# Joining a sort's sums on GpSimd between its scatters, instead of on VectorE

## The chip, the cores and the metric

One core of a Trainium2 chip. The metric is the device time of one execution in microseconds; of the kernel before three executions were timed, and one more was taken by the hardware profiler. All times inside the kernel are microseconds from the start of that profiled execution's span.

## The reference

A layer of a graph network over 3125 nodes of 256 values and 50000 edges. With xn = layernorm(x):

```python
# edges: src, dst (sorted by dst), one weight d2 for each
x   = cat(xn[src], xn[dst], d2)
msg = silu(layernorm(silu(x @ mW1 + mb1)) @ mW2 + mb2)
agg = segment_sum(msg, src)                      # messages summed by source node
h   = xn + silu(cat(xn, agg) @ uW1 + ub1) @ uW2 + ub2
x   = x + h + linear_attention(xn)               # q, k, v; k and v normalised
x   = x + top2_of_8_experts(layernorm(x))
```

The kernel sums the messages by source node on TensorE, and for that it must have the edges in the order of blocks of source nodes. The edges come sorted by dst. So there is a sort in front of everything else, and the change is in it.

## The kernel before

**Stages.** Up to 55 us: constants, loads, for each edge its place in the sorted order. Then the sort (L1581 on VectorE, L900 on TensorE, L1267 on ScalarE, L725 on GpSimd). Then the source tables (25 tiles: TensorE L885 to L887, ScalarE L1293, VectorE L1610), the key/value stage (25 tiles, from L961), mixing, the edge loop (up to 1150 us), the node update and the experts. Each engine has its own instruction list in a fixed order that is written out by hand; they meet by semaphores alone.

**The sort.** The 50000 edges lie on 125 partitions, 400 to each; they are taken in 16 groups (GROUPS) of 25 columns. For one group:

- VectorE compares (L1586, L1588) and multiplies (L1591, six products) and so makes one-hot matrices for lanes and for places, the latter times each of six values of an edge: dst in a high and a low part, the source row, and the weight in three bf16 parts. These six are the "pieces"; they are exact in bf16.
- TensorE sums 25 products into one PSUM bank (L906): now each edge's pieces stand at its sorted lane and place, 128 lanes x 28 places (PLACES), six times. It then makes the numbers of the chunks where the 7 runs (RUNS) of 128 chunks belong (L912): a product with two columns each, the high and the low part of a start.
- ScalarE copies the six pieces to SBUF (L1272, `pieces`, two sets in turn) and the source row, which is one piece only, straight to `sort_sb` (L1273, signal `sort_ok`).
- VectorE joins in `land(g - 1)`, behind the one-hot matrices of group g: dst = piece 0 + piece 1 (L1570), the weight = piece 3 + piece 4 + piece 5 (L1571, L1572), and the chunk numbers `chunk_to` = high part + low part + row (L1576, L1578, signal `chunk_ok`).
- GpSimd waits for `sort_ok` and `chunk_ok` of the group and issues 7 indirect DMAs (L729), each of which scatters 128 chunks of 48 bytes to DRAM by `chunk_to`; 112 in all.

**Order.** TensorE's bank of group g is free when `sort_ok` and `chunk_ok` of group g - 2 are there (L903). ScalarE's set of pieces is free when `chunk_ok` of group g - 2 is there (L1271). VectorE may overwrite its one-hot matrices when TensorE has summed group g - 2 (L1583). Beside the sort the same loop makes the normalised nodes, their transposes and the table of the destination nodes (two tiles a group; L922, L885 to L887, L840 on TensorE, L1221, L1279, L1285 on ScalarE, L1600 on VectorE).

**After it.** SP loads the scattered records back (L572) when all 112 scatters have landed and `logit0_ok` is there, a signal from tile 7 of the key/value stage (L1667). TensorE asks for the records behind the key/value stage. In the source tables TensorE may be four banks ahead of VectorE (L931); ScalarE waits for TensorE's signal `tab_ps` (L1292).

GpSimd does nothing between the last scatter and 370 us. From there it gathers rows for the edge loop with indirect DMAs too (L763), twelve at first, then four after each two small additions (L748, L750).

Of the kernel before, what the change touches and what calls it, by code (L numbers as in the profile page):

```python
# [4 lines left out]
F32 = mybir.dt.float32  # L5
# [37 lines left out]
def gps_layer(nc, x, src, dst, edge_weight1, mW1, mb1, ln_g, ln_b, mW2, mb2, uW1, ub1, uW2, ub2,  # L43
# [53 lines left out]
    with ctx:  # L97
# [11 lines left out]
        def at(name, shape, dt, owner, byte=0):  # L109

            return nc.alloc_sbuf_tensor_at(name, shape, dt, offset=place[owner] + byte)
# [92 lines left out]
        part_w = sort_use("part_w_t", [128, PLACES], F32)  # L204
        pieces = sort_use("pieces_t", [128, 2, PIECES, PLACES], F32)
# [82 lines left out]
        mixP_byte = filled["weights"] - 4 * QC * D  # L288
        k_n.append(at("k_n2", [128, NQ], F32, "weights", mixP_byte))
# [44 lines left out]
        run_to = s("run_to", [128, RUNS])  # L334
# [56 lines left out]
        def bank(b, n=512, rows=128, first=0):  # L391
# [16 lines left out]
        scattered, table_ps = sem("scattered"), sem("table_ps")  # L408
# [31 lines left out]
        gap_ok, exp_ok, hotk_ok, route_ps, tile_ok = (sem(n) for n in (  # L440
            "gap_ok", "exp_ok", "hotk_ok", "route_ps", "tile_ok"))
# [97 lines left out]
        def _(sp):  # L539
# [44 lines left out]
            sp.wait_ge(chunk_ps, GROUPS)  # L584
# [68 lines left out]
        def _(pool):  # L653
# [70 lines left out]
            pool.wait_ge(zeros_out, 16)  # L724
            for g in range(GROUPS):  # L725
                pool.wait_ge(sort_ok, g + 1)
                pool.wait_ge(chunk_ok, g + 1)
                for j in range(RUNS):
                    pool.indirect_dma_start(  # L729
                        out=sorted_edges, out_offset=bass.IndirectOffsetOnAxis(chunk_to[:, g, j:j + 1], 0),  # L730
                        in_=sort_sb[:, g, j].rearrange("p c f -> p (c f)"), in_offset=None).then_inc(scattered, 16)
# [106 lines left out]
        def _(pe):  # L838
# [61 lines left out]
            for g in range(GROUPS):  # L900
                pe.wait_ge(sort_in, SORT_IN * (g + 1))
                if g >= 2:
                    pe.wait_ge(sort_ok, g - 1)  # L903
                    pe.wait_ge(chunk_ok, g - 1)
                for c in range(GC):
                    m = pe.matmul(bank(g % 2, PIECES * PLACES), lane_hot_e[0:NP, g % 2, c // 2, :, c % 2],  # L906
                                  place_val[0:NP, g % 2, c // 2].rearrange("p v t b -> p (v t) b")[:, :, c % 2],
                                  start=(c == 0), stop=(c == GC - 1))
                m.then_inc(sort_ps, 1)
                pe.wait_ge(reached_ok, g + 1)  # L910
                for j in range(RUNS):
                    m = pe.matmul(bank(4 + g % 2, 2, first=2 * j), reached[0:NB + 1, g % 2, j * 128:j * 128 + 128],  # L912
                                  group_h[0:NB + 1, g, :], start=True, stop=True)
                m.then_inc(chunk_ps, 1)
                for t in TILES_OF[g]:
                    pe.wait_ge(fills, PADS)
                    pe.wait_ge(w_lo_ok, MW1_LO)
                    pe.wait_ge(xnT_lo_ok, t + 1)
                    if t >= 2:
                        pe.wait_ge(dst_sb, t - 1)  # L920
                    pe.wait_ge(fills, BW_CUT)
                    pe.matmul(bank(6 + t % 2, D), bw_sel[:], bw_cut[:], start=True, stop=False)  # L922
                    first_layer(bank(6 + t % 2, D), t, 1).then_inc(dst_ps, 1)
                for t in TILES_OF[g + 1]:
                    turn_xn(t)
# [299 lines left out]
        def _(act):  # L1225
# [41 lines left out]
            for g in range(GROUPS):  # L1267
# [3 lines left out]
                after(act, chunk_ok, g - 1)  # L1271
                A(pieces[:, g % 2].rearrange("p v t -> p (v t)"), bank(g % 2, PIECES * PLACES), ACT.Copy)  # L1272
# [145 lines left out]
            act.wait_ge(gap_ok, 1)  # L1418
            A(wtmp[0:NP], wtmp[0:NP], ACT.Exp).then_inc(exp_ok, 1)
# [49 lines left out]
        def _(dve):  # L1469
# [97 lines left out]
            def land(g):  # L1567
                dve.wait_ge(sort_ok, g + 1)
                piece = lambda v: pieces[:, g % 2, v].rearrange("p (j c) -> p j c", c=CHUNK)
                st.did(dve.tensor_tensor(sort_sb[:, g, :, :, 0], piece(0), piece(1), ALU.add))  # L1570
                step(dve.tensor_tensor(part_w[:].rearrange("p (j c) -> p j c", c=CHUNK), piece(3), piece(4), ALU.add))  # L1571
                st.did(dve.tensor_tensor(sort_sb[:, g, :, :, 2], part_w[:].rearrange("p (j c) -> p j c", c=CHUNK),  # L1572
                                         piece(5), ALU.add))
                dve.wait_ge(chunk_ps, g + 1)
                ends = bank(4 + g % 2, 2 * RUNS).rearrange("p (j h) -> p j h", h=2)
                st.did(dve.tensor_tensor(run_to[:], ends[:, :, 0], run_row[:], ALU.add))  # L1576
                st.join()
                dve.tensor_tensor(chunk_to[:, g], ends[:, :, 1], run_to[:], ALU.add).then_inc(chunk_ok, 1)  # L1578

            st.join()  # L1580
            for g in range(GROUPS):  # L1581
# [20 lines left out]
                if g:  # L1602
                    land(g - 1)
            land(GROUPS - 1)
# [247 lines left out]
            dve.tensor_tensor(wtmp[R], top_v[R, :, 1], top_v[R, :, 0], ALU.subtract).then_inc(gap_ok, 1)  # L1852
# [34 lines left out]
            dve.wait_ge(exp_ok, 1)  # L1887
# [118 lines left out]
```

## Time and profile before

| what | value |
|---|---|
| median of 3 runs | 1540.53 us (1538.51 to 1542.7) |
| profiled execution | 1532.65 us |
| its span, first to last instruction | 1530.9 us |
| TensorE, VectorE, ScalarE, GpSimd busy | 1302.3, 1154.1, 904.1, 866.8 us |
| granted clock of TensorE, mean | 0.918 |

The busy time of an engine is the time in which an instruction of it runs; the issue of a DMA by SP is not counted, an indirect DMA on GpSimd is, for as long as GpSimd makes its descriptors. In the timelines below a row is: start, duration, engine, line, operation, output<-inputs, shapes, and in brackets how long the engine was idle before it and what ended that ("issue": nothing that the profile shows; "remote": a signal whose sender it cannot name).

### The profile page before, as it was taken

What the parts mean: (1) busy time and instruction counts of PE and PEld (TensorE: products, weight loads), DVE (VectorE), ACT (ScalarE), POOL (GpSimd) and SP (SyncE); (2) the same over time, 40 slices, a digit from 0 to 9 for tenths busy, and PEclk for the clock granted to TensorE, in tenths of its full rate; (3) what the DMA queues carried; (4) which work ended last, traced back from release to release, by engine and by line L of the source; (5) the groups of instructions that cost most, each with busy time, mean ns of one, the idle gap of its engine ahead of it and who ended that gap; (6) DMA issues with size and microseconds to landing.
All of it is one profiled execution on the core that took longest, in us unless ns stands there. A gap on an engine that the chain in (4) does not pass through costs nothing.

```text
span 1530.9 us, 31977 instructions
## 1 busy us (share of the span) xinstructions
PE 1302.3 (85%) x8639; PEld 1135.4 (74%) x8640; DVE 1154.1 (75%) x2784; ACT 904.1 (59%) x1796; POOL 866.8 (57%) x960
## 2 busy tenths in 40 slices
PE   2576727998789999999999999999998956999991
PEld 1365626887678888888888888888886745888891
DVE  6975815884279989999999999999994678766662
ACT  1843603442257777777777777777774553666660
POOL 2287870002277777777777777777760012676761
PEclk7676967998879999999999999999999987999996
DMA  3911100001123333333333333333354143444447
GB/s 131 163 27 25 43 14 8 15 3 41 41 87 103 94 93 93 93 102 97 90 93 93 102 93 94 92 95 100 94 66 165 41 149 138 66 72 75 73 64 265
DMA packets 69786, 129.87 MB, mean 85 GB/s; under 512 B 22626, under 2 KB 43424, under 8 KB 69095
## 3 DMA queue, kind: packets, MB, share of 16 engines
q0 software_dynamic: 35408, 74.18, 20.5%
q1 hardware_dynamic: 33538, 51.70, 11.7%
q10 hardware_dynamic: 780, 3.24, 0.5%
q8 instruction: 31, 0.51, 0.1%
q14 instruction: 29, 0.24, 0.1%
HBM read 103.71 MB, written 25.22 MB: 84 GB/s over the span
## 4 chain that ended last, share of the span: by engine, by line
PE 51%; DVE 15%; ACT 11%; issue 10%; another core or an unknown queue 7%; DMA 3%; DVEq 1%; ACTq 1%; POOLq 0%; SPq 0%
PE ps L840 9%; ACT msg1n_t L1353 7%; PE ps L1079 5%; PE ps L1057 3%; PE ps L1052 3%; PE ps L1053 3%; PE ps L1069 3%; PE ps L1180 2%; DVE place_val_t L1591 2%; PE ps L1209 2%; PE ps L1211 2%; PE ps L1210 2%; PE ps L1181 2%; PE ps L1182 2%
## 5 line engine op out<-in xcount | busy, mean ns | idle before, releaser
L763 POOL DMA_INDIRECT msg_t<-dst_table,stage_idx x424 | 422.7, 997 | 121.1 <-issue 119.5
L1052 PE MATMUL ps<-w_hi_t,msg1T_hi_t 128*128 128x256 f32 x848 | 239.3, 304 | 0.0
L1353 ACT ACTIVATE msg1n_t<-msg_t,nw_b,nw_y 128x256 f32<-128x256 f32 x424 | 229.3, 591 | 0.0
L1079 PE MATMUL ps<-msg_t,hot_t 128*125 128x256 f32 x848 | 222.4, 384 | 2.0 <-issue 0.9
L1053 PE MATMUL ps<-w_lo_t,msg1T_hi_t 128*128 128x256 f32 x848 | 221.6, 283 | 0.0
L1360 ACT ACTIVATE msg_t<-ps 128x512 f32<-128x512 f32 x212 | 125.5, 592 | 124.0 <-remote 100.6
L1748 DVE TENSOR_TENSOR msg_t<-ps,msg_t 128x512 f32<-128x512 f32 x212 | 144.4, 681 | 63.3 <-remote 59.4
L1726 DVE TENSOR_TENSOR agg_t<-agg_t,ps 125x256 f32 x424 | 173.6, 409 | 6.8 <-PE ps L1079 3.4
L1057 PE MATMUL ps<-w_hi_t,msg1T_lo_t 128*128 128x256 f32 x848 | 171.0, 283 | 0.0
L1053 PEld LDWEIGHTS ps<-w_lo_t,msg1T_hi_t 128*128 128x128 f32 x848 | 163.1, 192 | 0.0
L1341 ACT ACTIVATE msg1T_hi_t<-ps 128x512 fp32r<-128x512 f32 x212 | 126.4, 596 | 60.4 <-PE ps L840 56.0
L1052 PEld LDWEIGHTS ps<-w_hi_t,msg1T_hi_t 128*128 128x128 f32 x848 | 161.9, 191 | 0.0
L1079 PEld LDWEIGHTS ps<-msg_t,hot_t 128*125 128x125 f32 x848 | 143.4, 187 | 21.0 <-issue 6.4
L840 PEld LDWEIGHTS ps<-ident,msg1n_t 128*128 128x128 f32 x848 | 97.4, 141 | 75.6 <-ACT msg1n_t L1353 52.4
L840 PE MATMUL ps<-ident,msg1n_t 128*128 128x128 f32 x848 | 134.6, 282 | 21.7 <-ACT msg1n_t L1353 19.1
L729 POOL DMA_INDIRECT sorted_edges<-sort_sb_t,chunk_to x112 | 128.0, 1143 | 37.3 <-issue 32.6
L1743 DVE BATCH_NORM_STATS2 est<-msg_t 128x6 f32<-128x512 f32 x212 | 147.5, 696 | 2.1 <-ACT msg_t L1346 2.1
L1735 DVE SCALAR_TENSOR_TENSOR msg1T_lo_t<-ps,msg1T_hi_t 128x512 fp32r<-128x512 f32 x212 | 144.4, 681 | 4.6 <-issue 2.4
L1346 ACT ACTIVATE msg_t<-msg_t 128x512 f32<-128x512 f32 x212 | 133.7, 631 | 12.4 <-DVE msg_t L1748 11.4
L1057 PEld LDWEIGHTS ps<-w_hi_t,msg1T_lo_t 128*128 128x128 f32 x848 | 132.1, 192 | 0.0
L1069 PE MATMUL ps<-src_hi_t,hotT_t 127*128 x424 | 114.3, 290 | 8.4 <-DVE hotT_t L1708 8.4
L831 POOL DMA_INDIRECT total<-slot_z,to_row x56 | 88.6, 1582 | 48.9 <-ACT slot_z L1433 44.3
(373 smaller groups left out, 3098.8 us busy)
## 6 DMA issues: line engine op xcount, KB each, us to landing
near_rows<-row_list SPq DMA_DIRECT2D x42, 320.0 KB
w_sb_t<-in_L_ffn_W_dram SPq DMA_DIRECT2D x16, 512.0 KB, 8.7
msg_t<-dst_table,stage_idx POOLq DMA_INDIRECT x424
res_t<-in_x_dram SPq DMA_DIRECT2D x1, 3125.0 KB
total<-zero_chunks_t SPq DMA_DIRECT2D x1, 3125.0 KB
dst_table<-dst_stage SPq DMA_DIRECT2D x25, 125.0 KB
xm_table<-xm_t POOLq DMA_DIRECT2D x5, 625.0 KB, 7.6
sum_a_t<-total SPq DMA_DIRECT2D x5, 625.0 KB, 10.7
```

The costliest lines, as they stand in the source:

```text
L763: pool.indirect_dma_start(out=msg1[:, k, j, :], out_offset=None, in_=dst_table, in_offset=bass.IndirectOffsetOnAxis(stage_idx[:, G * k + j ...
L840: return pe.transpose(out_, in_, ident[0:rows, 0:rows])
L1052: pe.matmul(o[j], part(msg1T_hi, j, c), w2_hi[:, c, :], start=(c == 0), stop=False)
L1053: pe.matmul(o[j], part(msg1T_hi, j, c), w2_lo[:, c, :], start=False, stop=False)
L1057: m = pe.matmul(o[j], part(msg1T_lo, j, c), w2_hi[:, c, :], start=False, stop=(c == KD - 1))
L1069: m = pe.matmul(bank(1 + k % 2, D, first=j * D), hotT[0:HR, k, j * 128:j * 128 + 128], table[0:HR, bass.ts(blk[k, j], 1), :].rearrange("p ...
L1079: m = pe.matmul(bank(7 * (kl % 2), D, rows=NP, first=j * D), hot[:, kl % 2, j, 0:NP], msg2[:, kl % 2, j, :], start=True, stop=True)
L1353: m = A(msg1n[:, (kl + 1) % 2, j, :], msg1[:, kk, j, :], ACT.Identity, bias=nw_b[:, kk, j:j + 1], scale=nw_y[:, kk, j:j + 1])
L1726: dve.tensor_tensor(a, a, bank(7 * ((k + 1) % 2), D, rows=NP, first=j * D), ALU.add).then_inc(sum_sb, 1)
L1735: dve.scalar_tensor_tensor(msg1T_lo[:, k % 2], bank(3 + k % 2), 1.0 / ROOT_D, msg1T_hi[:, k % 2].bitcast(F32), ALU.add, ALU.subtract).then ...
L1743: dve.bn_stats(est_pairs[:, kk, :], msg1[:, kk].rearrange("p j n -> p n j")).then_inc(spread_ok, 1)
L1748: dve.tensor_tensor(v, bank(1 + k % 2), v, ALU.add).then_inc(pre_sb, 1)
```

## The change

The three additions of `land` go from VectorE to GpSimd's list, between the scatters. For each group GpSimd runs three parts, one addition each; behind each part it issues scatters of earlier groups: 2, 2 and 1 up to group 8, from there 3, 4 and 3 (at most those of groups that are joined; so 3, 4, 1 in group 14, 3, 4, 0 in group 15, none in group 0), and at the end the last 7. A new semaphore `landed` counts joined groups. The pieces get six sets instead of two; ScalarE waits for `landed` of six groups ago instead of `chunk_ok` of two groups ago. The six sets lie where a later stage's `mixP` is; the third key buffer, which was there, moves to the start of that region. The high and the low part of the chunk numbers are summed by TensorE in PSUM (14 products of one column instead of 7 of two), and VectorE makes one addition of them instead of two. SP no longer waits for `chunk_ps`. Two semaphores of a much later stage (`gap_ok`, `exp_ok`) are made one.

```diff
-        part_w = sort_use("part_w_t", [128, PLACES], F32)
-        pieces = sort_use("pieces_t", [128, 2, PIECES, PLACES], F32)
+        part_w = at("part_w_t", [128, 2, PLACES], F32, "work", 15872)
+        PIECE_SETS = 6
...
+        pieces = at("pieces_t", [128, PIECE_SETS, PIECES, PLACES], F32, "weights", filled["weights"] - 4 * QC * D)
+        k_n.append(at("k_n2", [128, NQ], F32, "weights"))
...
@@ GpSimd
+            def land(g, part):
+                piece = pieces[:, g % PIECE_SETS]
+                if part == 0:
+                    pool.wait_ge(sort_ok, g + 1)
+                    st.did(pool.tensor_tensor(part_w[:, g % 2], piece[:, 3], piece[:, 4], ALU.add))
+                if part == 1:
+                    st.did(pool.tensor_tensor(sort_sb[:, g, :, :, 0], in_chunks(piece[:, 0]), in_chunks(piece[:, 1]), ALU.add))
+                if part == 2:
+                    st.join()
+                    pool.tensor_tensor(sort_sb[:, g, :, :, 2], in_chunks(part_w[:, g % 2]), in_chunks(piece[:, 5]), ALU.add)\
+                        .then_inc(landed, 1)
+
+            def scatter(g, j):
+                pool.wait_ge(landed, g + 1)
+                pool.wait_ge(chunk_ok, g + 1)
+                pool.indirect_dma_start(
+                    out=sorted_edges, out_offset=bass.IndirectOffsetOnAxis(chunk_to[:, g, j:j + 1], 0),
+                    in_=sort_sb[:, g, j].rearrange("p c f -> p (c f)"), in_offset=None).then_inc(scattered, 16)
+
+            sent = 0
             for g in range(GROUPS):
-                pool.wait_ge(sort_ok, g + 1)
-                pool.wait_ge(chunk_ok, g + 1)
-                for j in range(RUNS):
-                    pool.indirect_dma_start(
...
+                for part in range(3):
+                    land(g, part)
+                    upto = min(sent + (2 - part // 2 if g < 9 else 3 + part % 2), RUNS * g)
+                    for q in range(sent, upto):
+                        scatter(q // RUNS, q % RUNS)
+                    sent = max(sent, upto)
+            for q in range(sent, GROUPS * RUNS):
+                scatter(q // RUNS, q % RUNS)
@@ TensorE
                 for j in range(RUNS):
-                    m = pe.matmul(bank(4 + g % 2, 2, first=2 * j), reached[0:NB + 1, g % 2, j * 128:j * 128 + 128],
-                                  group_h[0:NB + 1, g, :], start=True, stop=True)
+                    for h in range(2):
+                        m = pe.matmul(bank(4 + g % 2, 1, first=j), reached[0:NB + 1, g % 2, j * 128:j * 128 + 128],
+                                      group_h[0:NB + 1, g, h:h + 1], start=(h == 0), stop=(h == 1))
@@ ScalarE
-                after(act, chunk_ok, g - 1)
-                A(pieces[:, g % 2].rearrange("p v t -> p (v t)"), bank(g % 2, PIECES * PLACES), ACT.Copy)
+                after(act, landed, g + 1 - PIECE_SETS)
+                A(pieces[:, g % PIECE_SETS].rearrange("p v t -> p (v t)"), bank(g % 2, PIECES * PLACES), ACT.Copy)
@@ VectorE
-            def land(g):
-                dve.wait_ge(sort_ok, g + 1)
-                piece = lambda v: pieces[:, g % 2, v].rearrange("p (j c) -> p j c", c=CHUNK)
-                st.did(dve.tensor_tensor(sort_sb[:, g, :, :, 0], piece(0), piece(1), ALU.add))
-                step(dve.tensor_tensor(part_w[:].rearrange("p (j c) -> p j c", c=CHUNK), piece(3), piece(4), ALU.add))
-                st.did(dve.tensor_tensor(sort_sb[:, g, :, :, 2], part_w[:].rearrange("p (j c) -> p j c", c=CHUNK),
-                                         piece(5), ALU.add))
+            def chunk_places(g):
                 dve.wait_ge(chunk_ps, g + 1)
-                ends = bank(4 + g % 2, 2 * RUNS).rearrange("p (j h) -> p j h", h=2)
-                st.did(dve.tensor_tensor(run_to[:], ends[:, :, 0], run_row[:], ALU.add))
-                st.join()
-                dve.tensor_tensor(chunk_to[:, g], ends[:, :, 1], run_to[:], ALU.add).then_inc(chunk_ok, 1)
+                dve.tensor_tensor(chunk_to[:, g], bank(4 + g % 2, RUNS), run_row[:], ALU.add).then_inc(chunk_ok, 1)
```

## Rows read from the trace of the kernel before

**Rows 1.** Stretches: PE, PEld, DVE, ACT, POOL busy (instructions), clock, DMA share, GB/s

```profile
100.00:165.00 65.00, 44.51 (x265) 36.86 (x265) 36.03 (x83) 25.97 (x57) 51.59 (x45) 0.70 0.11 27
165.00:198.00 33.00, 27.44 (x263) 23.81 (x261) 27.12 (x71) 17.55 (x40) 26.40 (x22) 0.97 0.16 40
198.00:240.00 42.00, 7.17 (x26) 5.99 (x27) 5.12 (x10) 3.13 (x9) 26.86 (x28) 0.53 0.06 10
257.00:352.00 95.00, 91.96 (x493) 78.16 (x492) 75.90 (x169) 44.35 (x74) 0.00 (x0) 1.00 0.03 10
```

**Rows 2.** Waits from 55 to 198 us (two) and from 198 to 300 us (one)

```profile
DVE xnT_lo_t L1600 <- issue: 26.9, 8, 5.9
...
ACT pieces_t L1272 <- remote: 24.2, 7, 4.9
...
ACT src_hi_t L1293 <- remote: 37.7, 5, 15.7
```

**Rows 3.** The chain that ended last, 216 to 257 us: start, duration, what

```profile
216.52 15.69 another core or an unknown queue
...
232.62 5.90 another core or an unknown queue
...
256.83 0.47 PE ps L961
```

**Rows 4.** Timeline of GpSimd: the first scatter, two in the sort, the last

```profile
71.34 1.95 POOL L729 DMA_INDIRECT sorted_edges<-sort_sb_t,chunk_to  x1 [3.45 <-DVE chunk_to L1578]
...
186.69 1.99 POOL L729 DMA_INDIRECT sorted_edges<-sort_sb_t,chunk_to  x1 [0.30 <-issue]
...
191.78 0.96 POOL L729 DMA_INDIRECT sorted_edges<-sort_sb_t,chunk_to  x1 [0.30 <-issue]
...
232.23 0.96 POOL L729 DMA_INDIRECT sorted_edges<-sort_sb_t,chunk_to  x1 [0.31 <-issue]
```

**Rows 5.** Timeline of VectorE in the sort, groups 6, 12, 14 and 15

```profile
98.64 1.88 DVE L1586 TENSOR_TENSOR lane_hot_e_t<-pair_iota_t,edge_h_t 125x3328 bf16<-125x3328 bf16 x1
...
166.76 1.88 DVE L1586 TENSOR_TENSOR lane_hot_e_t<-pair_iota_t,edge_h_t 125x3328 bf16<-125x3328 bf16 x1
...
179.56 1.88 DVE L1586 TENSOR_TENSOR lane_hot_e_t<-pair_iota_t,edge_h_t 125x3328 bf16<-125x3328 bf16 x1
...
185.27 0.18 DVE L1570 TENSOR_TENSOR sort_sb_t<-pieces_t 128x28 f32<-128x28 f32 x1
...
185.95 1.88 DVE L1586 TENSOR_TENSOR lane_hot_e_t<-pair_iota_t,edge_h_t 125x3328 bf16<-125x3328 bf16 x1
...
188.32 2.77 DVE L1591 TENSOR_TENSOR place_val_t<-place_hot_t,edge_h_t 125x728 bf16<-125x728 bf16 x6
...
196.27 0.17 DVE L1578 TENSOR_TENSOR chunk_to<-ps,run_to 128x7 int32<-128x7 f32 x1
```

**Rows 6.** Timelines: VectorE's six products of group 1, GpSimd's subtraction beside them

```profile
63.70 5.47 DVE L1591 TENSOR_TENSOR place_val_t<-place_hot_t,edge_h_t 125x728 bf16<-125x728 bf16 x6
...
64.39 2.52 POOL L722 TENSOR_TENSOR mw_lo_t<-mw_sb,mw_hi_t 128x1024 fp32r<-128x1024 f32 x1 [4.24 <-ACT mw_hi_t L1266]
```

**Rows 7.** Timelines: gather runs on GpSimd, and who waits at their end

```profile
374.11 0.97 POOL L763 DMA_INDIRECT msg_t<-dst_table,stage_idx  x1 [2.17 <-issue]
...
386.64 0.94 POOL L763 DMA_INDIRECT msg_t<-dst_table,stage_idx  x1 [0.30 <-issue]
...
388.32 0.42 DVE L1696 TENSOR_TENSOR res_t<-res_t,ps 125x256 f32<-125x256 f32 x1 [8.13 <-remote]
...
577.30 1.03 POOL L763 DMA_INDIRECT msg_t<-dst_table,stage_idx  x1 [0.17 <-issue]
...
582.27 0.21 POOL L748 TENSOR_TENSOR nw_v<-est,eps_sum 128x4 f32<-128x4 f32 x1
...
583.04 0.60 ACT L1360 ACTIVATE msg_t<-ps 128x512 f32<-128x512 f32 x1 [1.45 <-remote]
```

**Rows 8.** Timeline of SP: the load of the scattered records

```profile
293.40 0.25 SPq L572 DMA_DIRECT2D table_in_t<-sorted_edges  x1
```

More of the change, by code:

```diff
@@ L287, in gps_layer @@
         uw1_sb = at("uw1_sb", [128, KD, D], F32, "weights", filled["weights"] - 4 * QC * D)
-        mixP_byte = filled["weights"] - 4 * QC * D
-        k_n.append(at("k_n2", [128, NQ], F32, "weights", mixP_byte))
+        pieces = at("pieces_t", [128, PIECE_SETS, PIECES, PLACES], F32, "weights", filled["weights"] - 4 * QC * D)
+        assert 4 * PIECE_SETS * PIECES * PLACES <= 4 * QC * D
+        k_n.append(at("k_n2", [128, NQ], F32, "weights"))
         mixG_hi = w("mixG_hi", [128, KD, D], F32R)
@@ L333, in gps_layer @@
         run_row = s("run_row", [128, RUNS])
-        run_to = s("run_to", [128, RUNS])
         token = s("token", [128, TOPK * NB])
@@ L407, in gps_layer @@
             "reached_ok", "sort_in", "sort_ps", "sort_ok", "chunk_ps", "chunk_ok"))
-        scattered, table_ps = sem("scattered"), sem("table_ps")
+        scattered, landed, table_ps = sem("scattered"), sem("landed"), sem("table_ps")
         table_sb, side_out, xnT_lo_ok, w_hi_ok, w_lo_ok = (sem(n) for n in (
@@ L439, in gps_layer @@
             "var2_ok", "sd2_ok", "rstd2_ok", "xm_ok", "x2T_ps", "x2T_sb", "logit_ps"))
-        gap_ok, exp_ok, hotk_ok, route_ps, tile_ok = (sem(n) for n in (
-            "gap_ok", "exp_ok", "hotk_ok", "route_ps", "tile_ok"))
+        softmax_ok, hotk_ok, route_ps, tile_ok = (sem(n) for n in ("softmax_ok", "hotk_ok", "route_ps", "tile_ok"))
+        GAP_OK, EXP_OK = 1, 2
         logit_ok = sem("logit_ok")
@@ L583, in _ @@
             sp.wait_ge(chunk_ok, GROUPS)
-            sp.wait_ge(chunk_ps, GROUPS)
             sp.wait_ge(zeros_out, 16)
@@ L724, in _ @@
             pool.wait_ge(zeros_out, 16)
-            for g in range(GROUPS):
-                pool.wait_ge(sort_ok, g + 1)
-                pool.wait_ge(chunk_ok, g + 1)
-                for j in range(RUNS):
-                    pool.indirect_dma_start(
-                        out=sorted_edges, out_offset=bass.IndirectOffsetOnAxis(chunk_to[:, g, j:j + 1], 0),
-                        in_=sort_sb[:, g, j].rearrange("p c f -> p (c f)"), in_offset=None).then_inc(scattered, 16)
+            in_chunks = lambda t: t.rearrange("p (j c) -> p j c", c=CHUNK)
+            def land(g, part):
[16 more added lines that the diff above has]
+            sent = 0
+            for g in range(GROUPS):
+                for part in range(3):
[6 more added lines that the diff above has]
+                scatter(q // RUNS, q % RUNS)
             pool.wait_ge(table_sb, LOADS)
@@ L1417, in _ @@
                 copy_xm(t, t // 4 + 1)
-            act.wait_ge(gap_ok, 1)
-            A(wtmp[0:NP], wtmp[0:NP], ACT.Exp).then_inc(exp_ok, 1)
+            act.wait_ge(softmax_ok, GAP_OK)
+            A(wtmp[0:NP], wtmp[0:NP], ACT.Exp).then_inc(softmax_ok, 1)
             act.wait_ge(w2_in, 16 * NE)
@@ L1602, in _ @@
                 if g:
-                    land(g - 1)
-            land(GROUPS - 1)
+                    chunk_places(g - 1)
+            chunk_places(GROUPS - 1)
             dve.wait_ge(zeros_out, 16)
@@ L1851, in _ @@
             st.join()
-            dve.tensor_tensor(wtmp[R], top_v[R, :, 1], top_v[R, :, 0], ALU.subtract).then_inc(gap_ok, 1)
+            dve.tensor_tensor(wtmp[R], top_v[R, :, 1], top_v[R, :, 0], ALU.subtract).then_inc(softmax_ok, 1)
             for k in range(TOPK):
@@ L1885, in _ @@
             st.did(dve.tensor_copy(slot_t[R], slot_q[R, 1]))
-            dve.wait_ge(exp_ok, 1)
+            dve.wait_ge(softmax_ok, EXP_OK)
             step(dve.tensor_scalar(wgt[R, 0, :], wtmp[R], 1.0, None, ALU.add))
```

## The prediction

> **What bounds the kernel now.** I read the stretches first [rows 1]. The change touches nothing behind the key/value stage; all that can move lies before it, in the sort (56 to 196 us), the source tables (to 257 us) and the key/value stage (to 352 us). Two of the stretches are strange. From 198 to 240 us TensorE works 7.2 of 42 us, VectorE 5.1 and ScalarE 3.1, while GpSimd is the only engine that is never free (28 scatters). From 100 to 165 us VectorE too works only 36.0 of 65 us; in the 33 us behind it, with the same work in a group, 27.1.
>
> The waits say who is late [rows 2]. ScalarE waits 37.7 us in five waits for TensorE's signal that a source table is in PSUM; in the sort it waits 24.2 us for the pieces in the same way, and VectorE 26.9 us in front of L1600. The chain [rows 3] puts 15.69 us and 5.90 us of this on nobody ("another core or an unknown queue"): TensorE had long done the work. The signal itself is late, and it stays late as long as the scatters run: the last scatter starts at 232.2 us [rows 4], the chain moves again at 232.2 and 238.5 us and then at full speed, so that the key/value stage starts at 256.8 us.
>
> What the scatters do in those times is in GpSimd's timeline [rows 4]. Undisturbed, one starts every 1.265 us (0.96 busy, 0.30 between). While VectorE builds the one-hot tensors without a pause, a scatter now and then is held (1.99 us behind the 1.88 us comparison of L1586), four fit in a group of 6.4 us (179.56 to 185.95 us from one comparison to the next, [rows 5]), and nobody's signal is late. The same pattern comes back twice with the gathers [rows 7]: in the run that goes without a pause from 374.1 to 387.6 us VectorE waits 8.13 us, until 0.7 us after its end; and in the edge loop, where four gathers (577.3 to 582.3 us) are followed by two short GpSimd additions, ScalarE waits 1.45 us and gets its signal at 583.04, 0.8 us after the fourth. So my reading is: a run of indirect DMAs without a pause keeps TensorE's signals back from about the third or fourth on, and a pause lets them go. It also explains why the sort falls from 6.4 to 11 or 13 us a group: once VectorE idles, the scatters run without a pause, and that keeps VectorE idle.
>
> **The change, part by part.**
>
> *VectorE.* It loses the three piece additions and one of the two index additions. From the start of L1570 to the next comparison is 0.68 us [rows 5]; one instruction of some 0.15 us stays: 0.5 us a group saved. Against it, an addition on GpSimd that reads SBUF excludes VectorE's two-input instructions: beside the 2.52 us subtraction of L722 six products took 5.47 us [rows 6] instead of 2.77 [rows 5], the whole 2.5 us more. An addition of 28 elements lies between 0.21 us (4 elements, L748, [rows 7]) and 2.52 us (1024 elements); worked out along the line between them 0.26 us. Three a group give back 0.8 us. Net: 6.4 us becomes 6.5 us a group (bounds 5.9, if none is felt, and 7.2, if each costs double).
>
> The Trainium skill, "SBUF — State Buffer", section "Who interferes with whom", has a rule that speaks against the change: a VectorE instruction with two SBUF inputs and a GpSimd instruction that reads SBUF shut each other out for a whole instruction. The trace agrees, with the 5.47 us. By the rule alone, with nothing won at the signals, a group would be some 0.2 us longer and the kernel 3 us slower; that is the last rival below.
>
> *TensorE.* 14 products of one column for 7 of two in each group. No row here has one alone; they lie between nothing and, as the largest bound, the same again as all 44.5 us of TensorE's work shared over its 265 products [rows 1], 0.17 us each, 1.2 us for seven; they are far smaller than the mean product, so I take 0.3 us a group, under VectorE's 6.5 us, and nothing on the path where TensorE is not the bound (16 x 0.3 = 5 us if it were everywhere).
>
> *The sort's pace.* Between the comparisons of groups 6 and 12 there are 68.1 us (98.64 to 166.76, [rows 5]) for six groups; at 6.5 us 39 us: 29 us saved. TensorE's clock there averages 0.70, and 0.97 behind it [rows 1]; if it stayed low, TensorE would bound a group with its own 44.5 us of work in 65 us, or 7.8 us in each 11.35 us group, and 21 us would be left. I take 28: TensorE is busy most of the time when its signals aren't late, and had the high clock of 0.97 from 165 us on, at 6.4 us a group. The last index is then written at 168 us instead of 196.3 us [rows 5].
>
> *GpSimd's own chain.* Up to group 8 it sends five scatters and makes three additions a group: 5 x 1.265, 3 x (0.26 and a little more pause) = 7.2 us, and held by VectorE as now (6.4 less 4 x 1.265 us, so 1.3 us in each group) and at the additions, about 9.8 us. That is slower than the sort; the six sets of pieces are the buffer. Starting at about 75 us (group 0 sends nothing), group 8 is done at 153 us and group 9 is joined at about 162; the pieces of group 15, which need its set, come at 166. Just enough; at 11 us a group the sort would wait about 6 us. Then 72 scatters are left: 91 us, 21 additions 6 us, the waits on its own signal and VectorE's holds 7 us: end at about 257 us, against 233.2 now. The table load waits for that and for L1667; it is issued at 293.4 us now [rows 8] and TensorE asks for it only behind the key/value stage, 352 us. So the 24 us more of GpSimd are hidden, if the signals get through beside them.
>
> *The source tables.* Now 60 us; the 21 tables done when the signals are free take 18.3 us (238.5 to 256.83, [rows 3]), 25 take 22. The scatters now come in runs of 3, 4 and 3 with an addition between. As in the edge loop a signal is held up by 1 to 1.5 us in a run of four; four banks ahead hide part of it: I add 5 us. Key/value starts at 168 + 22 + 5 = 195 us, 62 us earlier.
>
> *The key/value stage.* It takes 95 us for 25 tiles [rows 1], TensorE busy for 92 of them: little slack. Until 257 us it now runs beside scatters, 16 tiles; a signal late by 1.45 us, as in the edge loop, for not quite every second tile is 0.6 us each, 10 us. The last seven scatters have no addition between them; by the run of twelve gathers that cost 8.1 us, some 4 us. Loss 14 us (bounds 3, if the delays fall where there is slack, and 26, if each tile loses 1.4 us).
>
> *The rest* (two semaphores made one, the third key buffer moved, the dropped wait of SP) changes no instruction on the path: nothing. Scatter waits added to each scatter are met before it and cost what the first scatter of a group pays today, no more than the others (0.30 us).
>
> Sum: 62 - 14 = 48 us. The profiled execution took 1532.65 us (span 1530.9 and 1.75 around it), so 1484.6; it is 7.9 us below the median of 1540.5, against which I state 1492.
>
> **The rivals.**
>
> *An addition is too short a pause* (slower). The release in the edge loop came 0.8 us behind the fourth gather, inside a break of 1.6 us; here the break is 0.17 + 0.26 us, little over the 0.30 us that a scatter leaves anyway. If it frees nothing, only GpSimd's wait on its own signal, once in ten scatters, does. From 168 us on the stage crawls until GpSimd ends at 257, and frees itself 5 us later (as 233.2 to 238.5 now). Six breaks of 3 us let 18 of the tables' 22 us pass; key/value starts at 266 us instead of 257: 1550, and up to 1564 if these breaks free nothing either. It decides as soon as signals pass in less than about a quarter of the time (22 of 89 us). The Trainium skill, "GPSIMD Engine Reference", section 4.1, says to leave elementwise additions to VectorE, about twice as fast; only this rival makes those 48 additions count, since then GpSimd's chain is the kernel's. Chance 0.18.
>
> *Half of it*: signals pass about half the time from 168 to 257 us. 45 us of work are done in 89, then 22 + 23 us of it lie behind at 257, so key/value in effect starts at 234: 23 us won, 1518. For it: the scatters' long run freed itself only 5.3 us behind its end (233.2 to 238.5), the run of twelve gathers after 0.7, so scatters seem to keep signals back more tightly. Chance 0.23.
>
> *The buffer runs dry*: at 11 us or more a group on GpSimd the sort ends 6 to 10 us later; 1500. Chance 0.06.
>
> *It isn't the scatters that keep the signals back*, but something of these stages: then only VectorE's part is left, from 4 us gained to 3 us lost. Against it: the three places above. 1540. Chance 0.05.
>
> *Forecast*: 1492, alone 1478 to 1506. Chance 0.48.
>
> **The numbers.** 0.3% is 4.6 us, about what a measurement here can tell. Faster: 0.48 + 0.23 + 0.06, less a little of the half case, 0.76; same 0.07; slower 0.17. The range of 8 in 10 runs from 1476 (sort at 5.9 us a group, tables without delay, a loss of 6 us: 16 us better than the sum) to 1545, into the slower case.
>
> **What the profile after would show.** Right: groups of some 6.5 us through the sort with the last L1578 near 168 us; L961 starting near 195; no wait of ScalarE at the tables over 2 us; GpSimd's last scatter near 257. Wrong: waits "remote" of 5 us and more between additions (first rival); the last scatter's end and the start of L961 close together (half); ScalarE waiting for GpSimd at L1272 (buffer); groups 6 to 11 at 8 us and more with a low clock.

## The result, and the profile after

The changed kernel takes 1551.84 us (median of 20 executions, 1546.93 to 1558.18) beside 1541.8 us for the kernel before (20, 1536.01 to 1553.66): ratio 1.0059, 95% interval 1.0043 to 1.0076, 10 us slower. The profiled execution has a span of 1550.6 us. I had forecast 1492.

The stretches of the changed kernel, columns as in [rows 1]:

```profile
100.00:165.00 65.00, 54.81 (x575) 47.54 (x576) 53.53 (x103) 39.82 (x88) 56.16 (x57) 0.95 0.16 43
165.00:198.00 33.00, 4.51 (x20) 3.72 (x18) 0.85 (x2) 1.15 (x3) 26.22 (x33) 0.55 0.07 12
198.00:240.00 42.00, 4.95 (x18) 4.07 (x18) 3.65 (x5) 1.15 (x3) 30.99 (x40) 0.50 0.03 5
257.00:352.00 95.00, 90.10 (x502) 77.51 (x503) 74.06 (x165) 45.21 (x79) 0.00 (x0) 1.00 0.03 10
```

The sort did what was forecast: in the first stretch VectorE is busy for 53.5 us where it had 36.0, TensorE for 54.8 where it had 44.5, at a clock of 0.95 instead of 0.70. Behind it everything all but stands still, from 165 us to GpSimd's end, twice as long as before. ScalarE's timeline in the source tables shows each signal of TensorE that came:

```profile
165.04 0.38 ACT L1246 ACTIVATE dst_stage<-ps 125x256 f32<-125x256 f32 x1 [4.11 <-remote]
172.57 0.38 ACT L1318 ACTIVATE src_hi_t<-ps 125x256 fp32r<-125x256 f32 x1 [7.15 <-remote]
185.17 0.38 ACT L1318 ACTIVATE src_hi_t<-ps 125x256 fp32r<-125x256 f32 x1 [12.22 <-remote]
201.27 0.38 ACT L1318 ACTIVATE src_hi_t<-ps 125x256 fp32r<-125x256 f32 x1 [15.72 <-remote]
218.07 0.38 ACT L1318 ACTIVATE src_hi_t<-ps 125x256 fp32r<-125x256 f32 x1 [16.42 <-remote]
234.87 0.38 ACT L1318 ACTIVATE src_hi_t<-ps 125x256 fp32r<-125x256 f32 x1 [16.42 <-issue]
247.53 0.38 ACT L1318 ACTIVATE src_hi_t<-ps 125x256 fp32r<-125x256 f32 x1 [12.27 <-remote]
253.16 1.21 ACT L1318 ACTIVATE src_hi_t<-ps 125x256 fp32r<-125x256 f32 x4 [5.25 <-remote]
```

That is six tables in 80 us, 13 to 17 us apart, and the others only behind GpSimd's end; before, five of these waits made 37.7 us [rows 2]. GpSimd's timeline at the start and at the end of that time:

```profile
164.13 0.26 POOL L731 TENSOR_TENSOR part_w_t<-pieces_t 128x28 f32<-128x28 f32 x1
164.56 0.98 POOL L742 DMA_INDIRECT sorted_edges<-sort_sb_t,chunk_to  x1 [0.17 <-issue]
165.84 0.97 POOL L742 DMA_INDIRECT sorted_edges<-sort_sb_t,chunk_to  x1 [0.30 <-issue]
167.11 0.96 POOL L742 DMA_INDIRECT sorted_edges<-sort_sb_t,chunk_to  x1 [0.30 <-issue]
168.09 0.26 POOL L733 TENSOR_TENSOR sort_sb_t<-pieces_t 128x28 f32<-128x28 f32 x1
...
177.29 0.26 POOL L731 TENSOR_TENSOR part_w_t<-pieces_t 128x28 f32<-128x28 f32 x1
...
240.71 0.98 POOL L742 DMA_INDIRECT sorted_edges<-sort_sb_t,chunk_to  x1 [3.90 <-remote]
...
248.32 0.96 POOL L742 DMA_INDIRECT sorted_edges<-sort_sb_t,chunk_to  x1 [0.30 <-issue]
```

Look at the gaps between scatters: an addition (0.26 us) and 0.16 us stand in the place of the 0.30 us that a scatter leaves anyway. Ten scatters and three additions take 13.16 us (from the row at 164.13 to that at 177.29), 1.315 us a scatter, against 1.265 without additions. The additions freed nothing. Even GpSimd's own signal, of its last addition, let it go on only after 3.90 us (0.28 us in e1_join below), and no table passed in that pause either. The last scatter starts at 248.3 instead of 232.2 us [rows 4], ScalarE goes on 3.9 us behind its end, and the key/value stage starts at 269.3 instead of 256.8 us [rows 3]:

```profile
269.30 0.47 PE L986 MATMUL ps<-wkvT_hi_t,xnT_hi_t 128*128 128x512 f32 x1 [1.13 <-DVE src_lo_t L1626]
```

So the sort gained 33 us (its last index at 162.9 instead of 196.3) and the tables lost 46: 12.5 us later in all, which agrees with the 10 us of the medians. (The two profiled executions differ by 19.7 us: that of the kernel before was 9 us under its median of 20. What is left lies behind the key/value stage, where the change touches nothing.)

### The profile page after: what moved, and what is told of

Same layout as the page of the kernel before. It is cut to its first block, busy times and chain, and to the rows that moved or that the text cites. A ratio compares the mean times of both kernels' runs of the same rounds, so it can differ in the third digit from the quotient of the medians.

```text
span 1550.6 us, 32278 instructions
## 1 busy us (share of the span) xinstructions
PE 1290.2 (83%) x8751; PEld 1124.7 (73%) x8752; DVE 1146.5 (74%) x2720; ACT 902.0 (58%) x1796; POOL 881.8 (57%) x1008
## 4 chain that ended last, share of the span: by engine, by line
PE 50%; DVE 15%; ACT 11%; issue 10%; another core or an unknown queue 10%; DMA 3%; DVEq 1%; ACTq 1%; POOLq 0%; SPq 0%
PE ps L864 8%; ACT msg1n_t L1378 7%; PE ps L1104 6%; PE ps L1082 3%; PE ps L1077 3%; PE ps L1078 3%; PE ps L1094 3%; DVE place_val_t L1607 3%; PE ps L1205 2%; PE ps L1234 2%; PE ps L1236 2%; PE ps L1235 2%; PE ps L1206 2%; PE ps L1207 2%
## 5 line engine op out<-in xcount | busy, mean ns | idle before, releaser
L742 POOL DMA_INDIRECT sorted_edges<-sort_sb_t,chunk_to x112 | 123.0, 1098 | 31.4 <-issue 26.6
```

## The experiments

The kernel before was measured again on nine further occasions, each on one core of some chip, beside the kernels below. On six of them it took 1404.2 to 1406.5 us, on three 1530.7 to 1543.8. Traces of both kinds tell what differs: I say "signals on time" and "signals late"; the first result above is of the late kind. 14 of the 18 runs met signals on time, four late ones. The four late ones stand on one execution each, but for h2_join_pace256 (four); what they gain is 60 us and more, where executions of one kernel lie within some 10 us (within 18 us in the first result).

**The kernel before and the changed one, unchanged** (signals on time).

> The kernel before, unchanged, for its trace on this chip. If the late signals belong to the chip and not to the program, a chip on which the kernel before takes about 1406 us shows no wait of ScalarE at the source tables over 1 us although the scatters run without a pause; then its key/value stage starts near 185 us instead of 256.8, and the stage behind the tables waits for nothing. If they belong to the program, the five waits of 4 us and more stand in every trace of it, also in a short one, and the 135 us are lost somewhere else.

> The changed kernel, unchanged. On a chip that does not hold the signals back there is nothing for the change to free and nothing that it can hold longer: the additions stand off VectorE's path (0.5 us in each of 16 groups, 8 us) and give 0.8 us a group back to it; my theory says within 5 us of the kernel before (1402 to 1411). On a chip like that of the first result: 10 us slower again, 1552. The rival, that the additions themselves cost the 10 us (GpSimd's port, VectorE's two-input instructions), says 10 us slower on either.

Measured beside a kernel before of 1404.8 us: b1_before 1409.6 (one execution), a1_after 1405.05, ratio 1.0000 (0.9991 to 1.0008). The stretch from 198 to 240 us of the kernel before:

```profile
198.00:240.00 42.00, 41.22 (x227) 35.33 (x226) 34.75 (x84) 19.42 (x33) 30.06 (x31) 1.00 0.04 6
```

and its row of the 25 tables (durations in ns: least, median, most; first and last start):

```profile
L1293 ACT ACTIVATE src_hi_t<-ps x25: 373/383/402, 168.3 to 188.8; 125x256 fp32r<-125x256 f32 x25
```

TensorE works 41.2 of 42 us where it worked 7.2 [rows 1], beside the same scatters, 1.26 to 1.51 us apart. The 25 tables take 20 us. So the late signals are no property of the program; where there is no wait to free, the two kernels are equal. The same row of the changed kernel:

```profile
L1318 ACT ACTIVATE src_hi_t<-ps x25: 373/383/402, 163.4 to 185.3; 125x256 fp32r<-125x256 f32 x25
```

It begins 5 us earlier (the execution of the kernel before in this comparison was 5 us over its median), though VectorE wrote its last index 13.8 us earlier, at 153.3 us. ScalarE's timeline shows why:

```profile
161.12 0.31 ACT L1297 ACTIVATE pieces_t<-ps 128x168 f32<-128x168 f32 x1 [9.48 <-POOL sort_sb_t L736]
```

Six sets of pieces are too few at five scatters a group, and that takes back what the shorter groups gave, as the next experiment shows. (In the first trace the same wait is there, 7.5 us up to 160.53, 0.1 us behind group 9's third addition at 160.18.)

**The additions back on VectorE** (all else of the change stays), signals on time.

```diff
-                    land(g, part)
...
+            def land_dve(g):
...
             def chunk_places(g):
+                land_dve(g)
```

> The changed kernel with the three additions of a group back on VectorE; one-column products, single index addition and six sets of pieces stay. GpSimd then sends nothing but scatters. If the additions between the scatters let the sort's signals through (groups of 5.9 us instead of 11), on a chip that holds signals back the sort falls back to 9 to 11 us a group and the time to about 1535 to 1545, as before; on a chip that does not, it is 1400 to 1410. If it is one of the other edits that speeds the sort up, the groups stay at 6 us on both.

1402.35, ratio 0.9988 (0.9976 to 1.0001); a second time (one execution) 1403.6 beside 1404.95 (again on time, so that its question stays open):

> The same kernel as e5_adds_back (the three additions back on VectorE), once more. Where signals are held back and it is the additions between the scatters that let the sort through: groups 7 to 12 take 9 us and more again, 1530 to 1550. If the sort keeps 6 us a group, one of the other edits (one-column products, single index addition) did that. The tables crawl in either case. Where they are not held back: 1402 again.

Groups of its sort take 6.27 us from comparison to comparison, those of the changed kernel 5.88 on average (92.60 to 145.49 for nine), those of the kernel before 6.4 us and more:

```profile
101.21 1.88 DVE L1611 TENSOR_TENSOR lane_hot_e_t<-pair_iota_t,edge_h_t 125x3328 bf16<-125x3328 bf16 x1
107.48 1.88 DVE L1611 TENSOR_TENSOR lane_hot_e_t<-pair_iota_t,edge_h_t 125x3328 bf16<-125x3328 bf16 x1
```

(the kernel with the additions back), and of the changed kernel:

```profile
98.48 1.88 DVE L1602 TENSOR_TENSOR lane_hot_e_t<-pair_iota_t,edge_h_t 125x3328 bf16<-125x3328 bf16 x1
104.42 1.87 DVE L1602 TENSOR_TENSOR lane_hot_e_t<-pair_iota_t,edge_h_t 125x3328 bf16<-125x3328 bf16 x1
```

So the three additions are worth 0.4 us a group on VectorE. But the tables start at 161.0 us with the additions back, 2.4 us earlier than in the changed kernel (163.4): its sort is 6 us longer (last index at 159.6 us), but no piece waits for GpSimd. Where signals are on time, the move buys nothing.

**GpSimd waits for its own signal behind every addition**, signals on time.

```diff
                         .then_inc(landed, 1)
+                    pool.wait_ge(landed, g + 1)
+                else:
+                    st.join()
```

> The changed kernel, but GpSimd waits for its own signal behind each of the 48 additions. Rate theory: the scatters, one in 1.27 to 1.32 us, overrun something that serves one in about 1.5 to 1.6 us; while it is behind, the signals of TensorE (and GpSimd's own) wait. Then each wait lasts until it has caught up, some 1 us after three or four scatters, TensorE's signals pass there, the source tables run, and L986 starts at 185 to 200 us instead of 269: 1490 to 1515 us. Break theory: nothing passes until about 4 to 5 us after the last scatter, however few there were before; then each wait is 4 us, GpSimd ends at about 330 us instead of 249 and the kernel takes 1540 to 1580 us. Third theory: only VectorE's dense comparisons keep the scatters harmless, pauses on GpSimd do nothing: 1552 us as now.

1405.64 beside 1406.51, ratio 0.9993 (0.9975 to 1.0010). The gap behind an addition becomes 0.28 us instead of 0.16; no signal was late that it could have freed, so it says nothing of the three theories in its expectation.

**A clear ahead of each scatter.** A `memset` of a scratch tile on GpSimd, 512 columns (0.5 us) or 256 (0.3 us), ahead of each scatter from the 42nd on; it waits for the clear two before it alone. Two further kernels put the same filler in lumps: e4_lump ten clears of 512 columns where `q % 10 == 0`, e6_break4 three where `q % 4 == 1`.

```diff
             def scatter(g, j):
+                q = g * RUNS + j
+                if q > 40:
+                    pause(512)
                 pool.wait_ge(landed, g + 1)
```

> The changed kernel with a memset of 512 elements on GpSimd (about 0.5 us) in front of each scatter from the 42nd on: one scatter in about 1.7 us instead of 1.32. Rate theory: that is slower than what serves them, so no signal is held, L986 starts at about 180 us, and the last scatter at about 272 us is what the table load waits for: 1465 to 1485 us. Break theory: breaks of 0.7 us free nothing, GpSimd ends 22 us later and the kernel takes 1570 to 1575 us. Third theory: 1570 to 1575 us too.

> The same with 256 elements (about 0.3 us): one scatter in about 1.47 us. Rate theory: near the rate at which they are served, so signals are late in part; between 1475 and 1530 us. Break and third theory: GpSimd ends 10 us later, 1560 to 1565 us.

> The changed kernel with the same pause as with 512 elements, but in one piece of about 5.3 us after every ten scatters from the 50th on. Rate theory: the scatters overrun again within each ten, and signals pass only in the break and the first two or three scatters after it, about a third of the time: L986 at 210 to 235 us, 1505 to 1530 us. Break theory: a break over 4 us frees the signals, for 1.3 us in each 18 us: 1555 to 1575 us. Third theory: 1575 us.

> The changed kernel with a break of three clears of 512 columns (0.5 us each, 1.6 us) ahead of every fourth scatter from the 41st on, 18 breaks, 29 us more on GpSimd. If a break of 1.6 us frees the signals, as in the edge loop, a chip that holds them back shows no wait of ScalarE over 4 us from 165 us on and gains 30 us and more against the changed kernel (1500 to 1520). If only a lower rate or the end of the run frees them, it is 25 to 30 us slower than the changed kernel (1575). On a chip that does not hold them back: only GpSimd's end is later, 0 to 15 us slower than before, as with the other pauses.

All four met signals on time, e6_break4 beside 1404.8, the others beside 1406.5: 1418.5 (ratio 1.0084), 1407.4 (1.0006), 1419.0 (1.0088), 1417.1 (1.0089). With no late signal to free they measure two other things. One is GpSimd's slack: with its last scatter at 264.4 us (256 columns) the clears cost nothing; with it at 278.8 us (512 columns), SP issues the load of the records only at 282.4 us, and ScalarE waits for it, 12 us in all:

```profile
ACT side_w_t L1350 <- DMA table_in_t<-sorted_edges: 11.2, 1, 11.2
```

The other is that clears in a row hold VectorE. In e6_break4 nobody waits for the load (last scatter at 273.6 us), yet from first to last tile (`kv_ss`) the key/value stage takes 101.1 us where the changed kernel takes 92.1; in e4_lump it takes 105.0. There an instruction of VectorE that takes 0.40 us otherwise lasts until the ten clears beside it are done; five such instructions cost 13 us in all. A row of GpSimd's timeline and one of VectorE's:

```profile
275.14 4.73 POOL L744 MEMSET scratch_t<- 128x512 bf16 x10
275.55 4.48 DVE L1662 TENSOR_SCALAR res_t<-res_t,res_scale,res_shift 125x256 f32<-125x256 f32 x1
```

The two kernels with a clear ahead of each scatter, once more:

> The same kernel as e2_pace512 (a clear of 0.5 us ahead of every scatter from the 41st on), once more, in the hope of a chip on which the kernel before takes about 1541 us. There, if a lower rate of scatters frees the signals, no wait of ScalarE is over 4 us from 165 us on and the time is 1490 to 1510; if only a whole pause of a microsecond and more or the end of the run does, it is 1570 to 1580. On a chip on which the kernel before takes 1405 us it is 1418 again and says nothing new.

> The same kernel as e3_pace256 (a clear of 256 columns ahead of each scatter from the 41st on: one scatter in 1.475 us instead of 1.315), once more. Where the kernel before takes about 1541 us: if the bound is a rate between 1.315 and 1.475 us a scatter, the waits of ScalarE at the source tables are all under 2 us and the time is 1465 to 1475, since GpSimd ends 14 us earlier than with the clear of 512 columns (1482); if it lies between 1.475 and 1.695 us, some signals are late by 5 us and more and it is 1500 to 1560. Where the kernel before takes 1405 us: 1407 again.

These met late signals: 1482.05 beside 1543.8 (1490 to 1510 was expected if a lower rate frees the signals), and 1464.5 beside 1530.7 (1465 to 1475 was expected). That the executions themselves were of the late kind is seen in their edge loops: from 560 to 900 us ScalarE waits 57.3 and 52.4 us for signals of a sender that the profile cannot name, 52.6 us in the kernel before of the first result, and no such wait is listed for b1_before and a1_after. In h1_pace512 the row of the tables:

```profile
L1329 ACT ACTIVATE src_hi_t<-ps x25: 377/384/406, 164.6 to 186.6; 125x256 fp32r<-125x256 f32 x25
```

and GpSimd's timeline:

```profile
220.61 0.97 POOL L753 DMA_INDIRECT sorted_edges<-sort_sb_t,chunk_to  x1 [0.17 <-issue]
221.58 0.54 POOL L744 MEMSET scratch_t<- 128x512 bf16 x1
222.28 0.97 POOL L753 DMA_INDIRECT sorted_edges<-sort_sb_t,chunk_to  x1 [0.16 <-issue]
```

In h3_pace256 the row of the tables:

```profile
L1329 ACT ACTIVATE src_hi_t<-ps x25: 373/383/402, 164.7 to 186.2; 125x256 fp32r<-125x256 f32 x25
```

and the stretch from 198 to 240 us:

```profile
198.00:240.00 42.00, 40.92 (x223) 34.98 (x223) 34.55 (x80) 19.77 (x34) 37.20 (x63) 1.00 0.03 5
```

With 512 columns the scatters start 1.66 us apart at the least, 2.0 in mean beside the tables and 1.76 behind them; with 256 columns 1.45 us at the least, 1.7 and 1.55 in mean. Neither holds anything back: the tables take 22 us with no wait of ScalarE over 1.8 us, and TensorE works 40.9 of 42 us behind them, although no break is longer than about 1 us. Scatters 1.315 us apart in mean (the changed kernel) hold nearly everything back. So what the additions lacked is room between the scatters. Not separated by these runs is whether the distance of neighbours counts, the mean over several scatters, or that something stands in every gap and not in three of ten.

**The kernel before with the same clears, and nothing of the change** (256 columns, from the 12th scatter on).

> The kernel before, with nothing of the change, and the clear of 256 columns (0.3 us) ahead of each scatter from the 12th on. Where signals are held back: if the scatters' rate is the whole cause, its sort goes at 6.4 us a group too, the tables and the key/value stage run through, and it is 1465 to 1480, as fast as the changed kernel with the same clears (1464.5); if the additions between the scatters are needed for the sort, groups stay at 9 to 11 us and it is 1490 and more. Where they are not held back: 1405 to 1410.

> The same kernel as b2_before_pace256 (the kernel before with a clear of 0.3 us ahead of each scatter from the 12th on), once more, where its first run met signals that were on time. Where the kernel before takes 1531 to 1544 us: 1465 to 1480 if the scatters' rate is the whole cause and nothing of the change is needed; 1490 and more, with groups of 9 to 11 us in the sort, if the additions between the scatters are.

With signals on time 1405.4, ratio 0.9999 (0.9981 to 1.0016). With late ones 1471.4 beside 1532.45 (one execution each), 61 us faster; 1465 to 1480 was expected if the scatters' rate is the whole cause. Its scatters are 1.45 us apart at the least, in mean 1.63 beside the tables and 1.50 behind them. Its tables:

```profile
L1303 ACT ACTIVATE src_hi_t<-ps x25: 374/384/407, 171.6 to 193.5; 125x256 fp32r<-125x256 f32 x25
```

Here the sort goes at 6.4 to 8.4 us a group from group 6 to group 12 (11.35 on average before [rows 5]) with all additions on VectorE. So of the 66 us by which h3_pace256 is faster than the kernel before, the room between the scatters alone gives some 61.

**Joins first: one scatter behind each addition** instead of up to four, so that the pieces' sets come free in time; then the same with the clear of 256 columns from the 46th scatter on.

```diff
-                    upto = min(sent + (2 - part // 2 if g < 9 else 3 + part % 2), RUNS * g)
+                    upto = min(sent + 1, RUNS * g)
```

> The changed kernel with one scatter instead of up to four behind each addition, so that GpSimd joins the pieces as they come and has more scatters left behind the sort. In the changed kernel group 15's pieces wait 7.5 to 9.5 us for the set of group 9, whose last addition stands behind four scatters (160.18, 160.53 us): six sets are too few at five scatters a group. Where signals are not held back: that wait is gone, the sort ends near 152 us, the tables start 8 to 10 us earlier, time 1394 to 1399 beside 1405. Where they are held back: the tables' signals still wait for the scatters' end, which does not move or moves 5 us earlier; 1545 to 1555. The rival for the first case, that GpSimd does not bound the sort, says 1405.

> Joins first, as in e7_join_first (one scatter behind each addition), and the clear of 256 columns ahead of each scatter from the 45th on. Where signals are held back: the sort ends 8 us earlier than in h1_pace512 and the tables run through; 1458 to 1470 if 1.475 us a scatter is slow enough, about 1530 to 1550 if not. Where they are not: 1400 to 1403, since GpSimd ends at about 265 us and so not much later than the 249 us that cost nothing.

e7_join_first, signals on time: 1400.7 beside 1405.7, ratio 0.9953 (0.9933 to 0.9972), 5 us faster; 1394 to 1399 was expected. ScalarE's wait for GpSimd is gone, but the tables start at 157.8 us, 5.6 earlier than in the changed kernel and not 8 to 10. h2_join_pace256, signals late: 1460.5 beside 1530.7, ratio 0.9532 (0.9509 to 0.9554), 70 us faster, the best version (1458 to 1470 was expected):

```profile
L1329 ACT ACTIVATE src_hi_t<-ps x25: 372/383/407, 160.5 to 182.8; 125x256 fp32r<-125x256 f32 x25
```

It was not run where signals are on time.

**Distance or mean rate.** e4_lump was to tell whether the mean over some tens of microseconds counts.

> The same kernel as e4_lump (ten clears of 512 columns, 4.9 us, behind each ten scatters), once more. GpSimd's work is that of h1_pace512 (1482 where the kernel before took 1544), in lumps. If the mean rate counts, it is 1480 to 1490 where signals are held back. If a backlog builds up within ten scatters 1.3 us apart, ScalarE waits 5 to 10 us for a table in each run and goes on in each break: 1515 to 1560. Where they are not held back: 1419 again.

> The same kernel as e4_lump and h5_lump, once more, where their runs met signals that were on time. Where the kernel before takes 1531 to 1544 us: 1480 to 1490 if the mean rate counts; 1515 to 1560, with waits of ScalarE of 5 to 10 us at the tables in each run of ten scatters, if a backlog builds up at 1.315 us a scatter and only runs off in the break.

This run, h5_lump before it (1418.2 beside 1404.95) and h7_lump after it (1420.5 beside 1405.1, the same expectation) all met signals on time; h6_lump took 1419.9 beside 1404.2. The question stays open. Two stretches of traces of the late kind bear on it, and not the same way. In the sort of the kernel before, from 166 to 192 us, the scatters start 2.3, 1.47, 1.34 and 1.3 us apart, again and again, 1.6 in mean, and no signal is late: two distances of four are about those of the changed kernel, and one of four is longer. In the edge loop four gathers start 1.27 us apart and then a break follows, 1.6 to 1.7 in mean, and ScalarE waits up to 2.0 us for single signals.

## Why the prediction was wrong

**The step that failed** is in "the source tables": "The scatters now come in runs of 3, 4 and 3 with an addition between. As in the edge loop a signal is held up by 1 to 1.5 us in a run of four [...]: I add 5 us." From the last index to the first product of the key/value stage it took 106.4 us instead of 27, so the term of 5 us came to 84. Behind it is the reading "a pause lets them go", which took any break for a pause. An addition adds 0.12 us (0.42 in place of 0.30) to three gaps in ten: 1.265 becomes 1.315 in mean, still too close. The places from which I had the reading have more room: 6.4 us for four scatters in the sort, 1.6 each [rows 5]; in the edge loop 6.5 us from the first gather of four (577.30 us, [rows 7]) to the first of the next (583.80 us), with 1.6 us free of gathers. The paced runs show it: with 1.6 to 1.7 us in mean beside the tables and 1.50 to 1.55 behind them nothing is late by more than 1.8 us, in the kernel before too.

**The first rival was right** in what it says of the break, "An addition is too short a pause". That its price came out, 1550 (1551.8 measured) with the key/value start at 266 us (269.3), is in part luck. It let 18 of the tables' 22 us pass in six breaks of 3 us, in which GpSimd waits for its own signal. There was one such wait, of 3.9 us, and no table passed in it; six tables passed one by one, between scatters, and 19 were left behind GpSimd's end, 16 us of work where it had 4. Against that GpSimd ended 8 us earlier than it said (249.3 instead of 257 us), and freed the signals 3.9 us behind its end, not 5.

**The sort** came out better than forecast: 5.9 us a group instead of 6.5, its last index at 162.9 instead of 168. The sum was also added up wrong: 6.4 less 0.5 and with 0.8 more is 6.7 us, not 6.5, and 7.5 where each addition costs double, not 7.2. Of its terms one held and one was off. The scatters of that time are held by VectorE and mixed with additions, 26 between 100.5 and 148.2 us, 1.9 us apart, and the signals were on time (right in direction; how much of it the additions did is open, see below). The 0.8 us a group that the additions were to take from VectorE were not taken: they wait themselves. Beside the 1.88 us comparison an addition took 1.74 us, bare 0.26:

```profile
130.64 1.74 POOL L731 TENSOR_TENSOR part_w_t<-pieces_t 128x28 f32<-128x28 f32 x1
132.54 1.09 POOL L742 DMA_INDIRECT sorted_edges<-sort_sb_t,chunk_to  x1 [0.16 <-issue]
```

The Trainium skill ("SBUF — State Buffer", "Who interferes with whom") says that the two shut each other out; here the trace agrees, but it is the addition on GpSimd, started 0.2 us behind the comparison, that pays the whole price, and it had slack for it. In [rows 6], where the subtraction was the long one, VectorE paid.

**The buffer** did run dry, which I had given 0.06: "Just enough", with the set of group 9 free at 162 us (160.2 measured), held only for a sort of 6.5 us a group; at 5.9 the pieces of group 15 were there at about 153 and waited 7.5 us, where signals are on time 9.5. Behind late signals I take it that it cost little, as the tables then wait for the scatters' end anyway; no run shows it apart.

**GpSimd's chain** was foreseen well: 9.7 us a group from group 1 to group 8 (73.2 to 150.8 us) where I had 9.8, end at 249.3 instead of 257. **The key/value stage** was not tested by the changed kernel, as no scatter ran beside it; in the four paced kernels that met late signals it starts at 184.0 to 194.6 us (195 was forecast for the changed one) and costs next to nothing beside the scatters: from its first to its last tile (`kv_ss`) 92.0 to 93.6 us, against 91.8 before, where I allowed for 14 more. But their scatters have more room than those that I had priced.

**What stays open**: what makes signals late on one occasion and not on another, and by what way an indirect DMA holds back a signal of TensorE. Chips with the numbers 9 and 11 gave both kinds; whether these numbers stand for the same chip each time isn't known. Whether the distance of neighbours or the mean counts, and whether a run of ten scatters 1.3 us apart may be made good by a long break. And the additions' part in late signals by itself: both runs with the additions back met signals on time.

## What to carry to other kernels

When engines idle with their work long done and the chain names nobody, look whether indirect DMAs are issued without a pause beside them, and work out their mean distance with and without the change: filler of 0.3 us on GpSimd, ahead of each, bought 61 us where 48 additions, in three gaps of ten, bought nothing at the signals. A break that helps at one place is no measure for a shorter one at another. Measure the kernel before several times, apart, before a gain is planned on its waits: here six of ten measurements had none of them. And when a faster stage hands its work to a slower engine, size the buffer by the faster pace, or let the slow engine take in before it gives out.

## What the runs showed of the hardware

- The same program took 1404 to 1407 or 1531 to 1544 us, 9% apart, on different occasions. In the late kind ScalarE waited up to 16.4 us for signals that TensorE gave while scatters were issued every 1.265 to 1.315 us (before, after), and no longer than 1.8 us at the tables where every gap was filled and they came 1.45 us apart at the least, 1.63 in mean or more there and 1.50 or more in the key/value stage, which ran at full pace (b3_before_pace256, h3_pace256, h1_pace512).
- The edge loop is slower in the late kind too: from GpSimd's clear of the sums to the end of the span it is 1118.3 us in h2_join_pace256 (340.9 to 1459.2) and 1069.4 us in a1_after (336.3 to 1405.7). Its waits from 560 to 900 us, in total, times, longest, of h2_join_pace256 and, below, of a1_after:

```profile
ACT msg_t L1397 <- remote: 56.4, 39, 1.9
DVE msg_t L1776 <- remote: 28.0, 41, 1.0
```

```profile
ACT msg1T_hi_t L1366 <- PE ps L864: 60.5, 104, 0.7
DVE agg_t L1742 <- issue: 10.9, 11, 1.4
```

So some 49 us more may be had there, perhaps by the same means, by spreading its four gathers; that wasn't tried.

- Single small GpSimd instructions are cheap between scatters: an addition of 28 elements takes 0.26 us bare, a clear of 256 columns 0.33, and both shorten the 0.30 us gap of the next scatter to 0.16.
- Many of them in a row are not: a VectorE `tensor_scalar` of 125x256 f32 (0.40 us) took 4.48 us beside ten clears of 512 columns (4.73 us) in e4_lump, and 0.55 us (median) beside single clears in e2_pace512.
